# Sixteen more attention steps transpose the probabilities by DMA, two weight loads get another gate, and a few instructions change places

## The chip, the cores and the metric

The kernel runs on one core of one Trainium2 chip. The metric is the device time of one execution in microseconds. The kernel before took 1331.49 us (median of 3 runs, 1330.44 to 1332.63). The execution that the profiler recorded took 1330.85 us, of which the profiled span is 1329.0 us.

## The reference

The input `x` has 8 batches of 128 tokens with 512 features, and a context of the same shape. Two layers follow each other, each with a cross attention and a feed-forward part:

```python
x = x + tanh(g_xattn[0]) * xattn_0(layernorm(x), ctx)   # 32 query heads, 8 key/value heads of 128
x = x + tanh(g_ffn[0])   * ffn_0(layernorm(x))          # blockwise 4- and 6-bit rounded weights and inputs
x = x + tanh(g_xattn[1]) * xattn_1(layernorm(x), ctx)
x = x + tanh(g_ffn[1])   * ffn_1(layernorm(x))          # int4 weights, permuted inputs, bias
```

Each attention projects q from the normalised `x` and k and v from the context, normalises each head of q and k (RMS), takes softmax(q k^T / sqrt(128) + mask) v, and multiplies the result with the output weights.

## The kernel before

**Steps.** One unit of attention is one group (one key/value head and its 4 query heads) of one batch. There are 2 x 8 groups x 8 batches = 128 units, and the kernel runs one step per unit, in a software pipeline: step n projects k, v and q of unit n, computes the scores and the softmax of unit n-1, turns the probabilities of unit n-2 and multiplies them with v, and multiplies unit n-3 with the output weights. Every projection is three products of two halves of a float (`three_products`, L1276): upper times upper, lower times upper, upper times lower.

**Stages.** `run_steps` gives each step a kind. FIRST is steps 0 to 7. QUANT is a loop over steps 8 to 47, which also quantises the feed-forward weights. ZONE is steps 48 to 87, written out one by one; there the order of the units is `ZONE_ORDER`, so that layer 0's feed-forward part can run between them. PLAIN is a loop over steps 88 to 119. LAST is steps 120 to 127, written out, and the drain behind it (steps 128 to 133), in which the last feed-forward part runs as well.

**The feed-forward part in the zone.** Steps 56 to 74 carry one tile (batch) of it in two steps, by the class `Tiles`: a `gate` step (odd) runs the gate and up products for columns 0 to 1023, and the `down` step behind it (even) the rest of them and the product with the down weights (L1448, 11 matmuls, written `ITILES`). The quantised input of a tile is transposed by a DMA from ACT's queue (`f_xqT`, L738), the hidden values by three DMAs (`f_iqT`, L685, for matmuls 0 to 3, 4 to 7 and 8 to 10). ACT issues both in the order of its program.

**Weights.** They arrive in two slots by DMA from SP's queue (`load_group`), and ACT and POOL split them into the halves (`split_upper` L710, `split_lower` L531). The tables `SPLIT_ZONE` and `SPLIT_ZONE_LATE` say which pieces are split in which step of the zone; pieces 0 to 5 of a group are q, k and v, pieces 6 to 9 are the output weights. In the zone the output weights of the next group wait for the slot (`y_ps`) and also for the third (or fifth) `f_iqT` of the last chunk, `iT_sb[2]` (L435). The q, k and v loads of the group after it stand behind them on SP.

**The transpose of the probabilities.** In FIRST, QUANT, ZONE and LAST, PE does it: four transposes into the bank `psPO` (`probabilities`, L1333), which ACT copies to `pT_hi` (L771), and DVE subtracts to `pT_lo` (L1012). In PLAIN a DMA does it. DVE scales the probabilities (L995) and copies their upper and lower 16 bits to two planes `p_planes` (L1002, two copies), SP issues the transpose (L498), ACT puts the upper halves back into `p_whole` (L762) and DVE the lower ones (L1007), ACT rounds `p_whole` to `pT_hi` (L766), and DVE subtracts (`probs_lower`). `by_dma(kind)` tells which way is taken. SP's loop `plain_group` has a load of q, k and v ahead of the group's first transpose and the load of the output weights behind the fourth.

**PE's order in a step.** k and v, q, (gate and up 2 in `down` steps), probabilities' transposes, scores (L1340), (gate and up 0), output (L1276), then `transposed()`: k's transpose (L1357) and q's four (L1268), then `values()` (L1369, three matmuls with `pT_hi` and `pT_lo`), and last gate and up 1 or the down product. In steps 124 on, `last_x` transposes the tile that is normalised for the last feed-forward part, right behind q; from step 125 `final` multiplies one tile behind `values`.

**DVE's order in a step.** In PLAIN: reciprocal (L986), scaling (L995), planes (L1002), `oT_lo` (L1065), `v_lo` (L1082), masked scores (L1109), `p_whole` (L1007), maximum (L990), q normalised (`scaled_q`, L1020), `pT_lo` (L1012), kT (L1135), x (L1147). In steps 124 to 127 the moments of a tile (L865) come behind `oT_lo` and its normalisation (L871) behind `v_lo`, and the scaling of the probabilities comes behind the moments. ACT copies that tile's transpose (`xT_hi`, L669) ahead of the normalised k (L699).

Of the kernel before, what the change touches and what calls it, by code (L numbers as in the profile page):

```python
# [4 lines left out]
FP32 = mybir.dt.float32  # L5
# [10 lines left out]
P = 128  # L16
# [51 lines left out]
LAST0 = ALL - BATCHES  # L68
END = ALL + 6
# [26 lines left out]
def step_of(group, b):  # L96
# [4 lines left out]
              13: ((C, 0), (C, 1)), 15: ((C, 4), (C, 5)), 17: ((C, 8), (C, 9)), 19: ((E, 2), (E, 3)), 21: ((E, 6), (E, 7)),  # L101
# [4 lines left out]
SPLIT_ZONE_LATE = {13: ((C, 2), (C, 3)), 15: ((C, 6), (C, 7)), 17: ((E, 0), (E, 1)), 19: ((E, 4), (E, 5)),  # L106
# [49 lines left out]
def flamingo_kernel(nc, x, ctxT, mask, g_xattn, g_ffn, norms, wq, wk, wv, wo, ffn_w,  # L156
                    packedT, scalesT, perm, bias, w4_rows, out):
    top = ExitStack()
    with top:
# [50 lines left out]
        p_turned = sb("p_turned", [P, 2 * KT, P], U16, under)  # L210
        p_whole = sb("p_whole", [P, D], FP32, under)
# [155 lines left out]
        def by_dma(kind):  # L367

            return kind == PLAIN

        def turned_by_pe(n):

            return n - 1 - (LAST0 - ZONE1 if isinstance(n, int) and n >= LAST0 else 0)

# [22 lines left out]
        def _(sp):  # L397
# [16 lines left out]
            def load_group(before, slot, q=None, freed=None, downs=None):  # L414
# [49 lines left out]
            load_group(B, 0, None, step_of(A, BATCHES - 1) + 1, 3)  # L464
            load_group(C, 1, None, step_of(B, BATCHES - 1) + 1, 5)
# [18 lines left out]
            def plain_group(before, slot):  # L484

                g, at = before + 1, slot * WSLOT
                for b in range(BATCHES):
                    unit = before * BATCHES + b - ZONE1
# [5 lines left out]
                    sp.wait_ge(planes_done, unit + 1)  # L494
                    sp.wait_ge(upper_placed, unit + 1)
                    sp.wait_ge(lower_placed, unit + 1)
                    sp.sem_inc(turning, 1)
                    sp.dma_start_transpose(p_turned[:, :, :], p_planes[:, :]).then_inc(planes_turned, 16)  # L498
# [3 lines left out]

            with sp.Fori(GROUPS // 2 + 1, GROUPS - 1) as h:
                plain_group(h * 2 + 1, 0)
                plain_group(h * 2 + 2, 1)
# [146 lines left out]
        def _(act):  # L652
# [59 lines left out]
            def step(n, b, kind, j, q=None):  # L712
# [19 lines left out]
                split_upper(late_pieces(n, kind))  # L732
                if calm(n, kind):
                    split_upper(split_pieces(n, b, kind, j))
# [23 lines left out]
                if has(n, 2) and by_dma(kind):  # L758

                    act.wait_ge(pv_ps, n - 2)  # L760
                    act.wait_ge(planes_turned, (n - ZONE1 + 1) * 16)
                    nc.scalar.activation(halves(p_whole[:, :])[:, :, 1], p_turned[:, 0:KT, :].rearrange("p k t -> p (k t)"),  # L762
                                         ACT.Copy).then_inc(upper_placed, 1)
                    act.wait_ge(upper_placed, n - ZONE1 + 2)
                    act.wait_ge(lower_placed, n - ZONE1 + 2)
                    nc.scalar.activation(pT_hi[:, :], p_whole[:, :], ACT.Copy).then_inc(pt_hid, 1)  # L766
                if has(n, 2) and not by_dma(kind):
# [52 lines left out]
                for k in gathered(n, kind):  # L820

                    act.wait_ge(w4_back, 16)
                    nc.scalar.activation(wp_hi[:, k, :], w4_turned[:, k, :], ACT.Copy).then_inc(wp_hid, 1)
# [29 lines left out]
        def _(dve):  # L853
# [151 lines left out]
            def place_lower(n):  # L1005
                dve.wait_ge(planes_turned, (n - ZONE1 + 1) * 16)
# [3 lines left out]
            def probs_lower(n, kind=None):  # L1010
                dve.wait_ge(pt_hid, n - 1)
                nc.vector.tensor_tensor(pT_lo[:, :], (p_whole if by_dma(kind) else psPO)[:, :], pT_hi[:, :].bitcast(FP32),  # L1012
# [28 lines left out]
            def step(n, b, kind, j, q=None):  # L1041
# [9 lines left out]
                if by_dma(kind):  # L1051
                    scaled_probs(n)
                    probs_planes(n)
# [23 lines left out]
                if has(n, 2) and not t.active and not by_dma(kind):  # L1077
                    scaled_probs(n)
                if has(n, 0):
# [4 lines left out]
                    if t.first is not None:  # L1084
                        ctx_lower(t.first)
# [468 lines left out]
```

## Time and profile before

| what | value |
|---|---|
| median of 3 runs | 1331.49 us |
| the profiled execution | 1330.85 us, span 1329.0 us |
| PE busy | 1315.4 us (99% of the span) |
| DVE busy | 979.3 us (74%) |
| ACT busy | 853.1 us (64%) |
| POOL busy | 624.9 us (47%) |
| share of PE in the chain that ended last | 90% |
| PE idle by the list of waits, longest | 3.9 us for `f_xqT`, 1.6 us at the start, 1.1 us for `f_iqT` |

Busy time counts a matmul from its start to a modelled end, so two that follow each other overlap. What one piece of work costs on PE is read from the distance between the starts of successive rows. The chain that ended last tells which engine set the end of the kernel, and the list of waits tells what an engine stood still for.

### The profile page before, as it was taken

How to read it: one execution, taken by the hardware profiler on the slowest of the kernel's cores; microseconds unless marked ns; L12 is line 12 of the kernel's file. 1: busy time of each engine (PE TensorE's matmuls, PEld its weight loads, DVE VectorE, ACT ScalarE, POOL GpSimd, SP SyncE). 2: the span in 40 equal slices, each digit the busy share in tenths (PEclk: the TensorE clock that was granted, in tenths of full speed). 3: DMA queues.
4: the chain of work that ended last, by engine and by line, in shares of the span. 5: the costliest groups of instructions: out<-in, count | busy, mean ns of one | idle time of the engine just before them, and what ended most of it. 6: DMA issues, size and time to landing. Idle time of an engine off the chain costs nothing.

```text
span 1329.0 us, 25509 instructions
## 1 busy us (share of the span) xinstructions
PE 1315.4 (99%) x7561; PEld 1113.1 (84%) x7561; DVE 979.3 (74%) x2055; ACT 853.1 (64%) x3339; POOL 624.9 (47%) x683
## 2 busy tenths in 40 slices
PE   8999999999999999999899999999999999999999
PEld 7888888888888888877677788888888888888887
DVE  6778787887878788688778857676767667675656
ACT  5767677676767676646566556666767667676542
POOL 2546565555555666357577534532333323232132
PEclk9999999999999999999999999999999999999999
DMA  8011211211121110021310012212232221320001
GB/s 295 1 60 51 68 49 26 74 38 63 50 66 51 66 51 27 5 67 23 95 51 16 20 48 68 92 64 64 57 80 55 58 54 53 79 55 16 1 9 56
DMA packets 83982, 73.90 MB, mean 56 GB/s; under 512 B 53185, under 2 KB 74561, under 8 KB 79809
## 3 DMA queue, kind: packets, MB, share of 16 engines
q1 hardware_dynamic: 66912, 67.46, 16.9%
q10 hardware_dynamic: 16672, 4.46, 1.6%
q0 software_dynamic: 320, 1.05, 0.2%
q8 instruction: 37, 0.61, 0.2%
q14 instruction: 41, 0.33, 0.1%
HBM read 57.48 MB, written 3.15 MB: 46 GB/s over the span
## 4 chain that ended last, share of the span: by engine, by line
PE 90%; DVE 4%; DMA 2%; POOL 2%; issue 1%; ACT 1%; SPq 0%; POOLq 0%; DVEq 0%; ACTq 0%
PE bank L1276 64%; PE bank L1340 8%; PE bank L1268 7%; PE bank L1369 7%; PE bank L1302 2%; PE bank L1357 1%; DMA f_iqT<-f_iq 1%; PE bank L1448 1%; DMA w_raw<-in_wv 1%; POOL rstd L560 0%; DMA f_xqT<-f_xq 0%; DVE f_q L955 0%; DVE amax L948 0%; POOL f_iq L586 0%; POOL probs L597 0%
## 5 line engine op out<-in xcount | busy, mean ns | idle before, releaser
L531 POOL TENSOR_TENSOR w_lo<-w_raw,w_hi (+1 forms) x150 | 196.7, 1327 | 150.5 <-ACT w_hi L710 150.5
L745 ACT ACTIVATE squares<-bank 128x128 bf16<-128x128 f32 x512 | 134.8, 279 | 197.7 <-PE bank L1276 197.4
L1109 DVE SCALAR_TENSOR_TENSOR probs<-bank,mask_sb 128x512 f32<-128x512 f32 x127 | 87.6, 690 | 191.0 <-PE bank L1340 173.5
L691 ACT ACTIVATE probs<-probs,negmax 128x128 f32<-128x128 f32 x512 | 198.2, 391 | 6.3 <-DVE negmax L990 3.8
L556 POOL TENSOR_TENSOR meansq<-sumsq,scalars 128x5 f32<-128x5 f32 x128 | 27.5, 215 | 370.5 <-ACT squares L745 370.5
L560 POOL TENSOR_TENSOR rstd<-meansq,scalars 128x5 f32<-128x5 f32 x128 | 153.1, 1196 | 10.9 <-POOL meansq L556 1.3
L1276 PE MATMUL bank<-w_hi,oT_hi 128*128 (+1 forms) x512 | 152.0, 419 | 0.0
L1276 PE MATMUL bank<-w_hi,xT_hi 128*128 (+1 forms) x512 | 141.2, 396 | 0.3 <-ACT w_hi L660 0.2
L1276 PE MATMUL bank<-w_hi,oT_lo 128*128 (+1 forms) x512 | 138.0, 391 | 0.0
L1276 PE MATMUL bank<-w_lo,oT_hi 128*128 (+1 forms) x512 | 137.9, 391 | 0.0
L1276 PE MATMUL bank<-w_lo,xT_hi 128*128 (+1 forms) x512 | 137.5, 390 | 0.1
L1276 PE MATMUL bank<-w_hi,xT_lo 128*128 (+1 forms) x512 | 137.0, 389 | 0.0
L1340 PEld LDWEIGHTS bank<-kT,qT 128*128 128x128 f32 x1024 | 130.5, 191 | 6.4
L1340 PE MATMUL bank<-kT,qT 128*128 128x128 f32 x1024 | 134.8, 274 | 0.0
L1276 PEld LDWEIGHTS bank<-w_lo,oT_hi 128*128 128x128 f32 x512 | 96.4, 188 | 22.0
L1276 PEld LDWEIGHTS bank<-w_lo,xT_hi 128*128 128x128 f32 x512 | 96.1, 188 | 21.9 <-DVE w_lo L884 0.7
L1276 PEld LDWEIGHTS bank<-w_hi,oT_lo 128*128 128x128 f32 x512 | 96.1, 188 | 21.2
L1276 PEld LDWEIGHTS bank<-w_hi,xT_lo 128*128 128x128 f32 x512 | 96.1, 188 | 19.9
L745 ACT ACTIVATION_READ_ACCUMULATOR squares<-bank 128x1 f32 x512 | 106.6, 208 | 0.0
L1276 PEld LDWEIGHTS bank<-w_hi,xT_hi 128*128 128x128 f32 x512 | 88.0, 189 | 13.2 <-ACT w_hi L660 1.4
L1276 PEld LDWEIGHTS bank<-w_hi,oT_hi 128*128 128x128 f32 x512 | 88.1, 191 | 12.7 <-issue 0.3
L691 ACT ACTIVATION_READ_ACCUMULATOR probs<-probs,negmax 128x1 f32 x512 | 97.3, 190 | 0.0
(129 smaller groups left out, 2986.0 us busy)
## 6 DMA issues: line engine op xcount, KB each, us to landing
w_raw<-in_wq SPq DMA_DIRECT2D x16, 1024.0 KB, 4.9
w_raw<-in_wo SPq DMA_DIRECT2D x16, 1024.0 KB, 4.9
fw_raw<-in_ffn_w SPq DMA_DIRECT2D x36, 192.0 KB, 2.3
w_raw<-in_wk SPq DMA_DIRECT2D x16, 256.0 KB, 5.3
w_raw<-in_wv SPq DMA_DIRECT2D x16, 256.0 KB, 5.5
x_sb<-in_x SPq DMA_DIRECT2D x7, 256.0 KB, 10.6
ctx_raw<-in_ctxT SPq DMA_DIRECT2D x7, 256.0 KB, 10.4
fw_raw<-in_ffn_w SPq DMA_DIRECT2D x7, 256.0 KB, 2.7
```

Of the source, the lines that this page charges most:

```text
L531: last = nc.gpsimd.tensor_tensor(lo, raw, hi.bitcast(FP32), ALU.subtract)
L556: nc.gpsimd.tensor_tensor(meansq[:, :], sumsq[:, :], eps_sb[:, :], ALU.add).then_inc(ms_done, 1)
L560: nc.gpsimd.tensor_tensor(rstd[:, :], meansq[:, :], minus_half[:, :], ALU.pow).then_inc(rs_done, 1)
L691: last = nc.scalar.activation(probs[:, h * P:(h + 1) * P], probs[:, h * P:(h + 1) * P], ACT.Exp, bias=negmax[:, h:h + 1], accum_out=rowsum ...
L745: last = nc.scalar.activation(squares[:, h // 2, (b + 1) % 4, h % 2, :], q_bank(n, kind)[:, h * P:(h + 1) * P], ACT.Square, scale=SCALE, a ...
L1109: nc.vector.scalar_tensor_tensor(heads(probs[:, :]), heads(psSQ[:, :]), SCALE, mask_sb[:, :].unsqueeze(1).to_broadcast([P, REP, P]), ALU.m ...
L1268: last = nc.tensor.transpose(dst[:, k * P:(k + 1) * P], src[:, k * P:(k + 1) * P], m)
L1276: last = nc.tensor.matmul(dst, left(a, k), right(b, k), start=(n == 0), stop=(n == len(terms) - 1))
L1302: last = nc.tensor.matmul(ps[:, 0:width], f_xqT[:, k, :], wT[:, col:col + width], start=(k == 0), stop=(k == KT - 1))
L1340: last = nc.tensor.matmul(psSQ[:, h * P:(h + 1) * P], qT[:, h * P:(h + 1) * P], kT[:, :], start=True, stop=True)
L1357: nc.tensor.transpose(kv_bank(n, kind)[:, 2 * P:3 * P], kn[:, :], ident[:, :]).then_inc(kt_ps, 1)
L1369: last = nc.tensor.matmul(psPO[:, :], v[:, slot, :], p[:, :], start=(k == 0), stop=(k == 2))
```

## The change

1. `DMA0 = ZONE1 - BATCHES` (step 80). `by_dma(n, kind)` is true for steps 80 to 127, so steps 80 to 87 (the end of the zone) and 120 to 127 (LAST) turn their probabilities by DMA as well. All counts that began at `ZONE1` begin at `DMA0`. SP runs `turning_group(E + 1, 1)` ahead of its loop and eight `turn_probs` behind it. A spacer moves `p_whole` off `f_s`.
2. PE's order in steps 80 to 127 is k's transpose, the values, q's transposes. DVE takes `probs_lower` ahead of `scaled_q` there.
3. In `down` steps of the zone `values()` stands between matmuls 7 and 8 of the down product.
4. The loads of the output weights for two groups of the zone wait for the fourth and the sixth `f_xqT`, not for the third and the fifth last `f_iqT`. Four pieces move: (C, 6) and (C, 7) from the late place of step 63 to step 65, (C, 8) and (C, 9) to the late place of 65, (E, 0) and (E, 1) from there to the late place of step 66.
5. The splits of the last feed-forward weights (`gathered`, steps 83 to 86) move from the end of the step to ahead of the scores on ACT and DVE, and the load of `w4_turned` moves on SP behind the transpose of step 81. The output weights that stood ahead of it now load behind the transpose of step 83.

```diff
+DMA0 = ZONE1 - BATCHES
-              13: ((C, 0), (C, 1)), 15: ((C, 4), (C, 5)), 17: ((C, 8), (C, 9)), 19: ((E, 2), (E, 3)), 21: ((E, 6), (E, 7)),
+              13: ((C, 0), (C, 1)), 15: ((C, 4), (C, 5)), 17: ((C, 6), (C, 7)), 19: ((E, 2), (E, 3)), 21: ((E, 6), (E, 7)),
...
-SPLIT_ZONE_LATE = {13: ((C, 2), (C, 3)), 15: ((C, 6), (C, 7)), 17: ((E, 0), (E, 1)), 19: ((E, 4), (E, 5)),
+SPLIT_ZONE_LATE = {13: ((C, 2), (C, 3)), 17: ((C, 8), (C, 9)), 18: ((E, 0), (E, 1)), 19: ((E, 4), (E, 5)),
                    21: ((E, 8), (E, 9))}
...
+        def by_dma(n, kind):
+            return kind == PLAIN or (isinstance(n, int) and DMA0 <= n < ALL)
...
-                    if downs is not None:
-                        sp.wait_ge(iT_sb[2], 16 * downs)
+                    if inputs is not None:
+                        sp.wait_ge(fxT_sb, 16 * inputs)
...
-            load_group(B, 0, None, step_of(A, BATCHES - 1) + 1, 3)
-            load_group(C, 1, None, step_of(B, BATCHES - 1) + 1, 5)
+            load_group(B, 0, None, step_of(A, BATCHES - 1) + 1, 4)
+            load_group(C, 1, None, step_of(B, BATCHES - 1) + 1, 6)
...
-            load_group(E + 1, 1)
-            sp.wait_ge(w4_scattered, 4 * 16)
-            sp.dma_start(w4_turned[:, :, :], w4_rows.rearrange("(k p) o -> p k o", p=P)).then_inc(w4_back, 16)
...
+            def turn_probs(n):
+                sp.wait_ge(planes_done, n - DMA0 + 1)
+                sp.wait_ge(upper_placed, n - DMA0 + 1)
+                sp.wait_ge(lower_placed, n - DMA0 + 1)
+                sp.sem_inc(turning, 1)
+                sp.dma_start_transpose(p_turned[:, :, :], p_planes[:, :]).then_inc(planes_turned, 16)
...
+                    turn_probs(before * BATCHES + b)
+                    if isinstance(before, int) and b == 1:
+                        sp.wait_ge(w4_scattered, 4 * 16)
+                        sp.dma_start(w4_turned[:, :, :], w4_rows.rearrange("(k p) o -> p k o", p=P)).then_inc(w4_back, 16)
...
+            turning_group(E + 1, 1)
             with sp.Fori(GROUPS // 2 + 1, GROUPS - 1) as h:
...
+            for n in range(LAST0, ALL):
+                turn_probs(n)
...
+                if by_dma(n, kind):
+                    probs_lower(n, kind)
                 if has(n, 2) and (t.gate is not None or calm(n, kind)):
                     probs_lower(n, kind)
...
-                if has(n, 0):
-                    transposed()
-                if has(n, 2):
+                if by_dma(n, kind):
+                    transposed_k()
+                    values()
+                    transposed_q()
+                elif has(n, 0):
+                    transposed_k()
+                    transposed_q()
+                if has(n, 2) and not by_dma(n, kind) and t.down is None:
                     values()
...
                     for k, (r, rows) in enumerate(ITILES):
+                        if k == CHUNKS[2][0] // P:
+                            values()
```

## Rows read from the trace of the kernel before

**Rows 1.** The page, part 1: busy us, share of span, instructions.
```profile
PE 1315.4 (99%) x7561; PEld 1113.1 (84%) x7561; DVE 979.3 (74%) x2055; ACT 853.1 (64%) x3339; POOL 624.9 (47%) x683
```

**Rows 2.** Waits of PE, whole span: us in total, times, longest us.
```profile
PE bank L1302 <- DMA f_xqT<-f_xq: 3.9, 1, 3.9
...
PE bank L1448 <- DMA f_iqT<-f_iq: 1.1, 1, 1.1
```

**Rows 3.** Timeline of PE, step 63: start us, us, engine, line, operation.
```profile
636.05 1.06 PE L1340 MATMUL bank<-kT,qT 128*128 128x128 f32 x8
...
646.17 1.07 PE L1276 MATMUL bank<-w_hi,oT_lo 128*128 128x512 f32 x4
```

**Rows 4.** Timeline of PE, step 65.
```profile
668.58 1.06 PE L1340 MATMUL bank<-kT,qT 128*128 128x128 f32 x8
...
673.04 1.07 PE L1276 MATMUL bank<-w_hi,oT_lo 128*128 128x512 f32 x4
```

**Rows 5.** Busy us by engine in a stretch, then granted clock, DMA share, GB/s.
```profile
643.10:646.20 3.10, 3.10 (x11) 2.46 (x10) 2.69 (x7) 1.41 (x8) 0.00 (x0) 0.63 0.00 0
```

**Rows 6.** Timeline of ACT and SP, step 63.
```profile
634.99 0.63 ACT L710 ACTIVATE w_hi<-w_raw 128x512 fp32r<-128x512 f32 x1 [1.39 <-DMA w_raw<-in_wo]
635.05 1.21 ACTq L738 DMA_TRANSPOSE f_xqT<-f_xq  x1
...
635.86 0.33 SPq L405 DMA_DIRECT2D w_raw<-in_wq  x1
```

**Rows 7.** The tile f_xqT: its 8 transposes, issue to landing.
```profile
DMA to landing us min/median/max: 2.4/2.4/5.9
```

**Rows 8.** Timeline of PE, a step whose probabilities PE transposes.
```profile
905.14 0.27 PE L1357 MATMUL bank<-ident,kn 128*128 128x128 f32 x1
...
905.61 0.48 PE L1369 MATMUL bank<-pT_hi,v_hi 128*128 128x512 f32 x1
905.92 0.39 PE L1369 MATMUL bank<-pT_lo,v_hi 128*128 128x512 f32 x1
...
906.38 0.65 PE L1276 MATMUL bank<-w_hi,ctx_hi 128*128 128x256 f32 x4
...
914.67 0.27 PE L1357 MATMUL bank<-ident,kn 128*128 128x128 f32 x1
```

**Rows 9.** Timeline of PE, a PLAIN step.
```profile
933.39 0.27 PE L1357 MATMUL bank<-ident,kn 128*128 128x128 f32 x1
...
934.00 0.50 PE L1369 MATMUL bank<-pT_hi,v_hi 128*128 128x512 f32 x1
...
934.80 0.63 PE L1276 MATMUL bank<-w_hi,ctx_hi 128*128 x4
...
942.60 0.27 PE L1357 MATMUL bank<-ident,kn 128*128 128x128 f32 x1
```

**Rows 10.** Timeline of ACT and DVE, the same PLAIN step.
```profile
932.10 0.63 ACT L766 ACTIVATE pT_hi<-p_whole 128x512 fp32r<-128x512 f32 x1 [0.32 <-DVE p_whole L1007]
...
932.65 0.69 DVE L1020 TENSOR_TENSOR qn<-bank,rstd 128x512 f32<-128x512 f32 x1
...
933.26 0.68 DVE L1012 TENSOR_TENSOR pT_lo<-p_whole,pT_hi 128x512 fp32r<-128x512 f32 x1
...
935.71 0.76 DVE L1002 COPY p_planes<-probs 128x512 uint16<-128x512 uint16 x2
```

**Rows 11.** The tile p_turned: ns min/median/max, first and last start; landing.
```profile
L762 ACT ACTIVATE p_whole<-p_turned x32: 787/799/820, 922.5 to 1208.0; 128x512 uint16<-128x512 uint16 x32
...
DMA to landing us min/median/max: 3.0/3.0/4.8
```

**Rows 12.** Timeline of DVE and PE, step 124.
```profile
1251.36 0.68 DVE L865 BATCH_NORM_STATS2 ln_stats<-x_sb 128x6 f32<-128x512 f32 x1
...
1253.57 0.55 DVE L871 TENSOR_SCALAR f_s<-x_sb,ln_mv,ln_rstd 128x512 f32<-128x512 f32 x1 [0.53 <-POOL ln_rstd L544]
...
1254.17 0.65 PE L1268 MATMUL bank<-ident,f_s 128*128 128x128 f32 x4
```

More of the change, by code:

```diff
@@ L365, in qn_first @@
             return kind == FIRST or calm(n, kind) or t.down is not None or t.next is not None
-        def by_dma(kind):
-            return kind == PLAIN
+        def by_dma(n, kind):
+            return kind == PLAIN or (isinstance(n, int) and DMA0 <= n < ALL)
         def turned_by_pe(n):
-            return n - 1 - (LAST0 - ZONE1 if isinstance(n, int) and n >= LAST0 else 0)
+            return n - 1 - (ALL - DMA0 if isinstance(n, int) and n >= ALL else 0)
         def halves(ap):
@@ L732, in step @@
                 split_upper(late_pieces(n, kind))
+                for k in gathered(n, kind):
+                    act.wait_ge(w4_back, 16)
+                    nc.scalar.activation(wp_hi[:, k, :], w4_turned[:, k, :], ACT.Copy).then_inc(wp_hid, 1)
                 if calm(n, kind):
@@ L1011, in probs_lower @@
                 dve.wait_ge(pt_hid, n - 1)
-                nc.vector.tensor_tensor(pT_lo[:, :], (p_whole if by_dma(kind) else psPO)[:, :], pT_hi[:, :].bitcast(FP32),
+                nc.vector.tensor_tensor(pT_lo[:, :], (p_whole if by_dma(n, kind) else psPO)[:, :], pT_hi[:, :].bitcast(FP32),
                                         ALU.subtract).then_inc(pt_lod, 1)
@@ L1076, in step @@
                     row_inverse(n)
-                if has(n, 2) and not t.active and not by_dma(kind):
+                if has(n, 2) and not t.active and not by_dma(n, kind):
                     scaled_probs(n)
@@ L1085, in step @@
                         ctx_lower(t.first)
+                for k in gathered(n, kind):
+                    dve.wait_ge(wp_hid, k + 1)
+                    nc.vector.tensor_tensor(wp_lo[:, k, :], w4_turned[:, k, :], wp_hi[:, k, :].bitcast(FP32),
+                                            ALU.subtract).then_inc(wp_lod, 1)
                 if t.first is not None:
@@ L1104, in step @@
                     dve.wait_ge(s_ps, n)
[L1105 to L1106 removed]
+                    if by_dma(n, kind):
+                        dve.wait_ge(planes_done, n - DMA0 + 1)
                     else:
@@ L1111, in step @@
                         mask_sb[:, :].unsqueeze(1).to_broadcast([P, REP, P]), ALU.mult, ALU.add).then_inc(masked, 1)
-                if by_dma(kind):
+                if by_dma(n, kind):
                     place_lower(n)
@@ L1115, in step @@
                     maximum(n)
+                if by_dma(n, kind):
+                    probs_lower(n, kind)
                 if has(n, 2) and (t.gate is not None or calm(n, kind)):
@@ L1125, in step @@
                     maximum(n)
-                if has(n, 2) and t.gate is None and not qn_first(n, kind, t):
+                if has(n, 2) and t.gate is None and not qn_first(n, kind, t) and not by_dma(n, kind):
                     probs_lower(n, kind)
@@ L1165, in step @@
                     int4_weights(n - INT4_0)
-                for k in gathered(n, kind):
-                    dve.wait_ge(wp_hid, k + 1)
-                    nc.vector.tensor_tensor(wp_lo[:, k, :], w4_turned[:, k, :], wp_hi[:, k, :].bitcast(FP32),
-                                            ALU.subtract).then_inc(wp_lod, 1)
                 if kind == LAST and n == LAST0:
@@ L1364, in values @@
                     pe.wait_ge(pt_lod, n - 1)
-                    if by_dma(kind):
+                    if by_dma(n, kind):
                         pe.wait_ge(o_lod, n - 2)
@@ L1385, in step @@
                     output()
-                    transposed()
+                    transposed_k()
+                    transposed_q()
                     values()
@@ L1412, in step @@
                     scores()
-                if has(n, 2) and not by_dma(kind):
+                if has(n, 2) and not by_dma(n, kind):
                     probabilities()
@@ L1433, in step @@
                     output()
-                if has(n, 0):
-                    transposed()
-                if has(n, 2):
+                if by_dma(n, kind):
+                    transposed_k()
+                    values()
+                    transposed_q()
+                elif has(n, 0):
+                    transposed_k()
+                    transposed_q()
+                if has(n, 2) and not by_dma(n, kind) and t.down is None:
                     values()
```

36 lines of the change are left out of this document (13 added, 23 removed).

## The prediction

> **What bounds the kernel now.** I read the page first, then the waits of PE, then the timelines of single steps. The page shows PE busy for 99% of the span and DVE, the next one, for 74% [rows 1]. So nearly every microsecond that PE saves comes off the end, and work that the change gives DVE or ACT is free until it makes PE wait. The waits of PE say how little idle time there is to win: one of 3.9 us for the transposed input of the feed-forward part, and one of 1.1 us for its hidden values [rows 2]. The rest must come from PE's own instructions. The working is therefore a comparison of step lengths, from k's transpose of one step to that of the next.
>
> **The stall in step 63.** From the scores to the last part of the output product takes 646.17 - 636.05 = 10.12 us in step 63 [rows 3] and 673.04 - 668.58 = 4.46 us in step 65 with the same work [rows 4]. The stall costs 5.66 us, more than the wait of 3.9 us. The clock shows the difference: after the idle time it is granted at 0.63 on average over 643.1 to 646.2, a mix of the 1.2 and the 2.4 GHz level, though PE is busy all through [rows 5]. Two things made the transpose late. ACT stood 1.39 us for the output weights ahead of it, and SP issued q's and k's weights 0.81 us after it [rows 6], and it took 5.9 us to land where the median is 2.4 us [rows 7]. The change takes away both: no piece is split at the late place of step 63, and the loads wait for this very transpose. It is then issued about 1.4 us earlier, near 633.6, lands by 636.0, and PE wants it at 636.05 + 0.9 = 637.0. What is late next is nothing within 1 us. The loads start near 636 and need some 6 us; the first transpose behind them is one step later, and the first consumer two steps later. The same holds for the second moved load. Taken: -5.6 us. Bounds: -1 us (only ACT's wait of 1.39 us goes) and -5.7 us.
>
> The four moved pieces are as many as before. In step 66 ACT gets two more of 0.6 us each [rows 6]. They fall between v and q's squares, where it waits for PE (ACT is busy for 64% [rows 1]), so I cost them at nothing. Without that cover the transposes behind them would be late by 1.2 us, the upper end.
>
> **Values inside the down product.** Eight steps. The eight matmuls ahead of the values now cover the wait for `pT_lo`, some 0.15 us as in a PLAIN step (below), but the step from bf16 to the split products, and back, is paid one more time. I take 0; bounds -1.5 and +1.5 us for the eight. The wait of 1.1 us in step 66 [rows 2] stays: the last three matmuls wait for the same landing, wherever the values stand.
>
> **PE's transposes of the probabilities.** From the first k and v product to k's next transpose is 914.67 - 906.38 = 8.29 us with them [rows 8] and 942.60 - 934.80 = 7.80 us without [rows 9]. So each of the 16 steps saves 0.49 us there, 7.8 us in all.
>
> **The new end of a step.** k's transpose to the first product of the next step takes 906.38 - 905.14 = 1.24 us where PE transposes [rows 8], and 934.80 - 933.39 = 1.41 us in PLAIN [rows 9]. The values begin 0.47 us after k's transpose in the one and 0.61 us in the other. The cause is `pT_lo`, which ends at 933.26 + 0.68 = 933.94, 0.06 us ahead of the values [rows 9, 10]. With `pT_lo` ahead of q on DVE it can start once `pT_hi` is there (932.10 + 0.63 = 932.73) and ends near 933.45. k's transpose takes 0.11 us, so the values start 0.14 us after it. q is then ready near 934.1, before the values end. The wait is gone but for 0.03 us.
>
> The new order has a price. The first values matmul behind q's transposes takes 905.92 - 905.61 = 0.31 us, and the next two 0.46 / 2 = 0.23 us each [rows 8]: the change from transposes to split products costs 0.08 us. The old order has it once, the new one twice (k's transpose to the values, q's transposes to the next product). I take 0.1 us for the second. The step's end is then 1.41 - 0.12 + 0.10 = 1.39 us. That is 0.02 to 0.03 us less than now in the 32 PLAIN steps (-0.9 us) and 0.15 us more than in a step with PE's transposes (16 x 0.15 = +2.4 us). Bounds: 0 and 0.2 us for the second change, that is -4.8 and +4.8 us over 48 steps.
>
> The Trainium skill (TensorE: Matmul & The Clock Gate, section Step-by-step: what each phase is for) says that the next weight load is pulled ahead of running matmuls, so that it overlaps them. By this rule the second change of kind is free, and the sum would be the rival at 1317.7 us below. The 0.08 us of the rows above speak against it for this pair of kinds; for a k and v product behind transposes no row exists.
>
> **What the DMA way adds to DVE, ACT and SP.** Two copies to planes (0.76 us) [rows 10], `p_whole`'s upper half on ACT (0.80 us) [rows 11] and its lower half. In PLAIN these fit a period of (1208.0 - 922.5) / 31 = 9.21 us [rows 11]. The planes end at 935.71 + 0.76 = 936.47, and 0.1 us for SP and 3.0 us later, at 939.6, the transpose lands. ACT begins `p_whole` at 932.10 - 0.32 - 0.80 = 930.98 [rows 10, 11], so a period later, at 940.2. That is 0.6 us of slack. The new order makes DVE 0.15 us later, and some 0.45 us remain. In steps 83 to 86 the gathered weights add 0.6 us on ACT and on DVE between v and the scores, where both wait for PE. The load of q, k and v stands ahead of the transpose of step 80 as in PLAIN. The first transpose took longer, 4.8 us [rows 11], and I expect 0.3 to 0.4 us for it again, at step 80 and no more at step 88. In straight-line code a few more transposes may be late: +0.4 us for the 16 steps. Bounds: -0.2 and +6 us.
>
> **Steps 124 to 127.** Here the order on DVE bites. The chain from moments to `last_x` on PE is 1254.17 - 1251.36 = 2.81 us, and PE starts 0.05 us after the normalisation ends (1253.57 + 0.55) [rows 12], so it has no slack. The DMA way puts the scaling (0.7 us, today behind the moments) and the planes (0.76 us [rows 10]) ahead of it, and starts DVE's step later. My estimate: DVE comes to the reciprocal 1.6 us after k's transpose of step 123, and gap, scaling, planes and `oT_lo` take 0.2 + 0.7 + 0.7 + 0.6 us, so the moments start at 3.8 us (today 2.7) and `last_x` is ready at 6.6 us. PE is there after 5.5 to 5.6 us, as today: a wait of 1.0 us. In step 125, with `xT_lo` ahead as well, it is 1.1 to 1.2 us. Steps 126 and 127 have 2.7 us of final products ahead and hide it. ACT's copy of the turned tile now stands between `pT_hi` and k, which makes k's transpose some 0.3 us late in each of the four steps. Together +3.3 us; bounds 0 and +6 us.
>
> **The sum.** -5.6 (step 63), 0 (down steps), -7.8 (transposes), +2.4 and -0.9 (new end of a step), +0.4 (late landings), +3.3 (steps 124 to 127), and -0.4 for the later start that moves from step 88 to step 80 and its partly smaller price: -8.6 us. On the profiled execution's 1330.85 us that is 1322.3 us. The median of the runs is 0.6 us above that execution; I forecast 1322.5 us.
>
> **Rivals.**
> 1. The second change of kind is free. For it: weight loads overlap elsewhere. Against it: the 0.08 us of rows 8. Then 48 x 0.1 us less, 1317.7 us.
> 2. The input's transpose in step 63 stays late, because a wait other than the weights holds ACT or the loads find another transpose to delay. Against it: its landing is at the median wherever no load runs beside it. Then only some 1 us of 5.6 us comes, and the time is 1327 us; with the last steps at their upper bound 1330 us.
> 3. Slower: the DMA transposes in the 16 straight-line steps land late. The slack is about 0.45 us over 3.0 us; each further microsecond is PE's. At the 4.8 us of the worst one [rows 11] a step loses 4.8 - 3.45 = 1.35 us, 16 steps 21.6 us, and the time is 1322.5 + 21.6 - 0.4 = 1343.7 us. It decides from a mean landing near 4.0 us, where 16 x 0.55 us eat the gain. Against it: the median is 3.0 us, and the 1.5 MB of loads ahead of a group's first transpose do not move it.
> 4. The values or q's transposes wait in the new order because `pT_hi` comes from ACT later than I read. At 0.15 us a step, 48 steps cost 7 us: 1329.5 us, no measurable change.
>
> **Chances.** The forecast 0.60, rival 1 0.18, rival 2 0.09, rival 3 0.05, rival 4 0.08. What a measurement can tell from no change is 0.2%, 2.7 us, so "faster" is below 1328.8 us. The forecast and rival 1 are faster, rival 2 half of the time or more: 0.86 with a part of rival 4. Within 0.2%: 0.09. Slower: 0.05. The range of 8 in 10 goes from 1316 us, past rival 1, to 1328 us.
>
> **What would show it.** The wait of PE for `f_xqT` is gone and the clock is full throughout. Steps 80 to 86 and 120 to 122 are 9.15 to 9.20 us long instead of 914.67 - 905.14 = 9.53 [rows 8], and PLAIN's 9.17 to 9.21. The first k and v product behind q's transposes takes 0.08 us or more over its group of today. PE waits for `f_s` in steps 124 and 125. The prediction is wrong if PLAIN's step falls below 9.12 us or rises above 9.25 us, if the last steps lose nothing, or if `p_turned` has a median landing above 3.4 us.

## The result and the profile after

| | before | after |
|---|---|---|
| median of 6 runs, us | 1330.68 (1329.57 to 1332.63) | 1326.87 (1325.66 to 1327.81) |
| ratio to before, 95% interval | | 0.9969 [0.9956, 0.9982] |
| profiled execution: span, us | 1329.0 | 1325.3 |

The change made the kernel 3.8 us (0.3%) faster. That lies in the forecast range (1316 to 1328 us), but it is less than half of the 8.6 us of the sum. The page of the changed kernel, part 1, answers to [rows 1]:

```profile
PE 1308.3 (99%) x7497; PEld 1103.1 (83%) x7497; DVE 994.0 (75%) x2103; ACT 864.3 (65%) x3355; POOL 623.2 (47%) x683
```

PE has 64 transposes less and is busy 7.1 us less, yet the span shrank by only 3.65 us (1329.00 to 1325.35): PE now waits more. The waits of PE (us in total, times, longest) answer to [rows 2]:

```profile
PE bank L1469 <- issue: 3.6, 7, 0.5
PE bank L1367 <- ACT kn L707: 2.4, 4, 1.0
PE bank L1497 <- POOL ident L530: 1.6, 1, 1.6
PE bank L1278 <- DVE f_s L879: 1.3, 2, 0.8
...
PE bank L1381 <- DVE pT_lo L1020: 0.6, 2, 0.3
...
PE bank L1469 <- DMA f_iqT<-f_iq: 0.4, 1, 0.4
```

The wait of 3.9 us for `f_xqT` is gone. In its place stand a wait called "issue" ahead of the down product, seven times 0.5 us, and waits for `kn`, `f_s` and `pT_lo`. The wait for `f_iqT` fell from 1.1 to 0.4 us in this execution, but that is no finding: in e3 and e4, which have the same code in the zone, it is 1.0 us and none.

The difference in step lengths says what each stretch gave. The length of step n runs from its own transpose of k to that of step n+1, so it holds the rest of step n and most of the work of step n+1:

| steps | forecast, us | measured, us |
|---|---|---|
| 0 to 56 | 0 | +0.27 |
| 56 to 79 (step 63, down steps) | -5.6 | -3.25 |
| 79 to 88 (8 new DMA steps) | -2.7 | -3.10 |
| 88 to 119 (PLAIN) | -0.9 | +0.19 |
| 119 to the end (8 new DMA steps) | +0.6 | +2.16 |
| start of the span | 0 | +0.08 |
| sum | -8.6 | -3.65 |

The late landings (+0.4) and the late first transpose (-0.4) of the forecast cancel and stand in no line. The readings behind this table follow.

**Step 63.** Timeline of PE (start us, us), which answers to [rows 3], and the transposed input's landing, to [rows 7]:

```profile
636.88 1.06 PE L1350 MATMUL bank<-kT,qT 128*128 128x128 f32 x8
637.77 1.89 PE L1312 MATMUL bank<-wT,f_xqT 128*128 128x512 bf16 x8
...
641.34 1.07 PE L1286 MATMUL bank<-w_hi,oT_lo 128*128 128x512 f32 x4
```
```profile
DMA to landing us min/median/max: 2.4/2.4/2.5
```

From the scores to the last part of the output product are now 641.34 - 636.88 = 4.46 us, as in the undisturbed step of [rows 4], where [rows 3] had 10.12 us. The stretch from the scores to k's transpose runs at the full clock (0.63 before [rows 5]), though DMA is busy for 0.91 of it:

```profile
636.88:642.25 5.37, 5.37 (x31) 3.96 (x30) 4.18 (x7) 3.90 (x19) 2.61 (x4) 1.00 0.91 316
```

**A step with a down product (64).** DVE and PE, start, length, and in brackets the idle time before:

```profile
655.08 0.68 DVE L1020 TENSOR_TENSOR pT_lo<-bank,pT_hi 128x512 fp32r<-128x512 f32 x1
...
655.31 0.63 PE L1278 MATMUL bank<-ident,qn 128*128 128x128 f32 x4
655.68 0.68 DVE L885 TENSOR_TENSOR xT_lo<-bank,xT_hi 128x512 fp32r<-128x512 f32 x1
656.46 1.89 PE L1469 MATMUL bank<-wT,f_iqT 128*128 128x512 bf16 x8 [0.52 <-issue]
658.00 0.58 PE L1381 MATMUL bank<-pT_hi,v_hi 128*128 128x512 f32 x1
```

The down product writes the bank from which DVE still subtracts to get `xT_lo`. PE starts 0.10 us after that subtraction ends (655.68 + 0.68 = 656.36). The view names no engine for this semaphore and calls the time "issue". Before, the values products stood between q's transposes and the down product, and their 0.8 us covered the wait. That `xT_lo` is what PE waits for is inferred here from the two times; e1 and e2 test it.

**A written-out step with the DMA way (83).** Timeline of PE, which answers to [rows 8]:

```profile
871.94 0.30 PE L1367 MATMUL bank<-ident,kn 128*128 128x128 f32 x1
872.01 0.47 PE L1381 MATMUL bank<-pT_hi,v_hi 128*128 128x512 f32 x1
...
872.78 0.60 PE L1278 MATMUL bank<-ident,qn 128*128 128x128 f32 x4
873.14 0.72 PE L1286 MATMUL bank<-w_hi,ctx_hi 128*128 128x256 f32 x4
873.70 0.64 PE L1286 MATMUL bank<-w_lo,ctx_hi 128*128 128x256 f32 x4
874.17 0.64 PE L1286 MATMUL bank<-w_hi,ctx_lo 128*128 128x256 f32 x4
...
881.03 0.29 PE L1367 MATMUL bank<-ident,kn 128*128 128x128 f32 x1
```

The step takes 881.03 - 871.94 = 9.09 us, against 9.53 us in [rows 8]. The first four k and v products behind q's transposes take 873.70 - 873.14 = 0.56 us, the next four 0.47 us: the second change of kind costs 0.09 us. In e5 the same four products stand behind the values and take 865.82 - 865.34 = 0.48 us, so the price comes from what stands ahead of them and not from their being the first:

```profile
865.34 0.65 PE L1284 MATMUL bank<-w_hi,ctx_hi 128*128 128x256 f32 x4
865.82 0.64 PE L1284 MATMUL bank<-w_lo,ctx_hi 128*128 128x256 f32 x4
```

A PLAIN step takes 9.18 us, against 9.21 us in [rows 9]:

```profile
1002.13 0.27 PE L1367 MATMUL bank<-ident,kn 128*128 128x128 f32 x1
1002.24 0.50 PE L1381 MATMUL bank<-pT_hi,v_hi 128*128 128x512 f32 x1
...
1011.31 0.27 PE L1367 MATMUL bank<-ident,kn 128*128 128x128 f32 x1
```

**Step 124.** PE, POOL, DVE and ACT, which answer to [rows 12]:

```profile
1247.47 0.66 PE L1278 MATMUL bank<-ident,f_s 128*128 128x128 f32 x4 [0.53 <-DVE f_s L879]
...
1249.62 1.29 POOL L653 TENSOR_TENSOR x_sb<-x_sb,bias_sb 128x512 f32<-128x512 f32 x1
1249.66 1.57 DVE L1015 COPY p_whole<-p_turned 128x512 uint16<-128x512 uint16 x1
1251.33 0.63 ACT L778 ACTIVATE pT_hi<-p_whole 128x512 fp32r<-128x512 f32 x1 [2.54 <-DVE p_whole L1015]
1252.76 0.33 PE L1367 MATMUL bank<-ident,kn 128*128 128x128 f32 x1 [0.98 <-ACT kn L707]
```

The wait for `f_s` is there, at half the forecast size. Larger is one that the forecast did not have: DVE's copy of the turned tile's lower half takes 1.57 us where its median is 0.46 us. It starts 0.04 us after POOL's addition of the bias and ends 0.32 us after it (1249.62 + 1.29 = 1250.91; 1249.66 + 1.57 = 1251.23). `pT_hi`, k and k's transpose come late behind it. Step 123 to 124 takes 11.46 us instead of 10.09, step 124 to 125 11.70 instead of 10.15.

**Late landings.** Where a turned tile lands late, ACT shows it (step 95):

```profile
981.33 0.79 ACT L774 ACTIVATE p_whole<-p_turned 128x512 uint16<-128x512 uint16 x1 [1.07 <-DMA p_turned<-p_planes]
...
983.09 0.33 PE L1367 MATMUL bank<-ident,kn 128*128 128x128 f32 x1 [0.38 <-ACT kn L707]
```

The two lengths around such a landing both grow, the first because k waits and the second because the values start late. Steps 85 and 86 take 9.57 and 9.50 us, 0.48 and 0.40 us more than the steps ahead of them; steps 94 and 95 take 9.74 and 9.87 us, 0.57 and 0.69 us more than theirs. The landing of the 48 transposes is otherwise as in [rows 11]:

```profile
DMA to landing us min/median/max: 3.0/3.0/4.7
```

### The profile page after: what moved, and what is told of

Read it like the earlier page. It is cut to its first block, busy times and chain, and to the rows that moved or that the text cites. A ratio compares the mean times of both kernels' runs of the same rounds, so it can differ in the third digit from the quotient of the medians.

```text
span 1325.3 us, 25509 instructions
## 1 busy us (share of the span) xinstructions
PE 1308.3 (99%) x7497; PEld 1103.1 (83%) x7497; DVE 994.0 (75%) x2103; ACT 864.3 (65%) x3355; POOL 623.2 (47%) x683
## 3 DMA queue, kind: packets, MB, share of 16 engines
q10 hardware_dynamic: 16672, 4.46, 1.6%
## 4 chain that ended last, share of the span: by engine, by line
PE 88%; issue 5%; DVE 3%; POOL 1%; DMA 1%; ACT 1%; SPq 0%; POOLq 0%; ACTq 0%; DVEq 0%
PE bank L1286 62%; PE bank L1350 8%; PE bank L1278 7%; PE bank L1381 7%; PE bank L1312 2%; PE bank L1469 1%; PE bank L1367 1%; DMA p_turned<-p_planes 1%; POOL rstd L568 1%; DMA w_raw<-in_wv 1%; DVE probs L1122 0%; DVE pT_lo L1020 0%; ACT pT_hi L778 0%; DVE w_lo L892 0%; DVE p_whole L1015 0%
## 5 line engine op out<-in xcount | busy, mean ns | idle before, releaser
L539 POOL TENSOR_TENSOR w_lo<-w_raw,w_hi (+1 forms) x150 | 194.0, 1309 | 162.4 <-ACT w_hi L718 162.4
L568 POOL TENSOR_TENSOR rstd<-meansq,scalars 128x5 f32<-128x5 f32 x128 | 156.0, 1219 | 10.8 <-POOL meansq L564 1.1
```

What stands on the lines that cost most here:

```text
L539: last = nc.gpsimd.tensor_tensor(lo, raw, hi.bitcast(FP32), ALU.subtract)
L568: nc.gpsimd.tensor_tensor(rstd[:, :], meansq[:, :], minus_half[:, :], ALU.pow).then_inc(rs_done, 1)
```

## The experiments

Every median below is of 4 to 11 runs (e9: 4, e5: 11). The kernel before ran beside them, with medians of 1330.84 us (beside e1 to e4), 1330.69 us (e5 to e8) and 1330.08 us (e9, e10), and ratios are to it. Kernels of different groups are therefore compared by what each gained on the kernel before beside it. The 95% intervals of most ratios overlap with the change's, so what one edit did is read from the step lengths of the traces. Those have a spread of their own: the sum of steps 56 to 74 differs by up to 1.1 us between traces with the same code there (238.4 us in the change and e4, 239.5 us in e3), most of it in step 58, while steps 60, 62, 64, 70 and 72 agree within 0.03 us. Line numbers in a kernel move by up to 7 where lines were added; e6 has those of the kernel before.

**e6: the moved loads and splits alone.** The kernel before, with `SPLIT_ZONE`, `SPLIT_ZONE_LATE` and the wait of the change:

```
-                        sp.wait_ge(iT_sb[2], 16 * downs)
+                        sp.wait_ge(fxT_sb, 16 * inputs)
```

> The kernel before with the moved loads and pieces of the zone alone (the wait for the fourth and sixth input transpose, the tables of the splits). Theory: the whole stall of step 63, 5.1 to 5.7 us, is this part's, and nothing of it needs the DMA way: 1330.8 - 5.4 = 1325.4 us, and the interval 62 to 63 falls from 19.5 to 13.9 us. Rival (the moved loads meet another transpose): a new wait for f_iqT or f_xqT of over 1 us shows in steps 64 to 68, and the gain is under 4 us.

Measured: 1325.58 us, 0.9961 [0.9947, 0.9976]. The stretch from k's transpose of step 62 to that of step 63 falls from 19.50 to 13.84 us, by 5.66 us. The wait for `f_xqT` is gone, and one wait of 0.9 us for `f_q` came behind k's transpose of step 67, one step behind the place to which two of the pieces moved:

```profile
PE bank L1302 <- DVE f_q L955: 0.9, 1, 0.9
```

Steps 56 to 74 give 4.84 us together. This one edit carries a gain of about 5 us. The rest of the change gave nothing in sum: against e6 the trace of the change is 1.6 us longer from step 56 to 79, 3.1 us shorter from 79 to 88 and 2.2 us longer behind step 119. The edit moves the loads and the pieces together, so how much of the stall each of the two caused is not separated.

**e1: the values ahead of the down product again.**

```
-                if has(n, 2) and not by_dma(n, kind) and t.down is None:
+                if has(n, 2) and not by_dma(n, kind):
                     values()
-                        if k == CHUNKS[2][0] // P:
-                            values()
```

> The changed kernel with the values ahead of the down product again, as before. Theory: in the changed kernel the down product writes the bank that DVE still reads for xT_lo, and without the values ahead of it PE waits 0.5 us for that in each of the seven down steps that also have a next tile; those steps fall from 14.3 to 14.4 us to 13.9 us, and the time by 3.5 us, to about 1323.4 us. Rival, the time is lost in the three changes between bf16 and split products inside the down product: then step 58, which has no next tile, loses as well, the wait labelled issue remains in part, and the step falls by 0.2 us, the time by 1.5 us.

Measured: 1324.89 us, 0.9952 [0.9939, 0.9966], 2.0 us less than the change. The wait called "issue" is gone from PE's list, and steps 56 to 74 are 2.46 us shorter (3.5 us expected). The down steps 60, 62 and 64 take 13.84 us instead of 14.37 to 14.38, the steps behind them 13.06 instead of 12.92. PE in step 64:

```profile
654.15 0.63 PE L1278 MATMUL bank<-ident,qn 128*128 128x128 f32 x4
654.66 0.50 PE L1381 MATMUL bank<-pT_hi,v_hi 128*128 128x512 f32 x1
...
655.46 2.55 PE L1467 MATMUL bank<-wT,f_iqT 128*128 128x512 bf16 x11
```

**e2: the values stay inside, DVE takes `xT_lo` ahead of `pT_lo`.** This takes away the wait and keeps the order of the change on PE:

```
+                if t.next is not None and t.down is not None:
+                    xT_lower(BATCHES + t.next)
                 if has(n, 2) and qn_first(n, kind, t) and not calm(n, kind):
                     probs_lower(n, kind)
-                if t.next is not None:
+                if t.next is not None and t.down is None:
                     xT_lower(BATCHES + t.next)
```

> The changed kernel with one exchange on DVE in down steps: xT_lo of the next tile ahead of pT_lo. The values stay inside the down product. Theory (PE waits for xT_lo): the wait of 0.5 us shrinks to under 0.1 us, down steps fall to 13.8 to 13.9 us, the time by 3 to 3.6 us, to about 1323.5 us. Rival (the cost is the change of kind inside the down product): down steps keep 14.3 us and the time stays at 1326.9 us.

Measured: 1324.94 us, 0.9955 [0.9941, 0.9968]. DVE and PE in step 64:

```profile
653.67 0.68 DVE L885 TENSOR_TENSOR xT_lo<-bank,xT_hi 128x512 fp32r<-128x512 f32 x1
...
653.90 0.63 PE L1280 MATMUL bank<-ident,qn 128*128 128x128 f32 x4
...
654.27 0.68 DVE L1020 TENSOR_TENSOR pT_lo<-bank,pT_hi 128x512 fp32r<-128x512 f32 x1
654.45 1.89 PE L1471 MATMUL bank<-wT,f_iqT 128*128 128x512 bf16 x8
```

The product starts 0.55 us after q's transposes began, without a gap. Steps 56 to 74 are 3.00 us shorter than in the change and 0.54 us shorter than in e1; its down steps 60, 62, 64 and 70 take 13.76 to 13.80 us, those of e1 13.84 us. So the cost was the wait for `xT_lo` and not the extra changes between bf16 and the split products: with the wait gone, the values inside are the slightly better place. e2's time is no better than e1's because one more transpose landed late in it, the one of step 84 (4.45 us): steps 79 to 87 are 1.2 us longer than in the change and 0.6 us longer than in e1.

**e3: PE transposes the probabilities again from step 124 on.**

```
-            return kind == PLAIN or (isinstance(n, int) and DMA0 <= n < ALL)
+            return kind == PLAIN or (isinstance(n, int) and DMA0 <= n < LAST0 + 4)
```

The count of PE's own transposes and SP's loop go with it.

> The changed kernel with the DMA way for steps 80 to 123 alone; steps 124 to 127 transpose on PE again, with the order of before. Theory: steps 124 and 125 lose 2.9 us in the changed kernel against before, the two behind them and the drain about 0.8 us, all by DVE's planes and POOL's bias; they come back: 1326.9 - 3.5 = 1323.4 us, and the intervals 123 to 124 and 124 to 125 return to 10.1 us. Rival (the loss comes from what lies ahead of step 124, a late transpose or the new end of a step): the two intervals stay over 11 us.

Measured: 1323.62 us, 0.9945 [0.9932, 0.9959]. Step 119 to the end of the span is 117.7 us long, against 120.7 us in the change and 118.6 us before. The DMA way in the last four steps thus costs 3 us against PE's. The two stretches named in the expectation take 10.66 and 10.16 us; the first stays 0.6 us above the 10.1 us, with a wait of 0.46 us for `f_s` in it.

**e4: POOL's addition of the bias waits for `pT_lo`.** The DMA way stays in the last steps; only what runs beside DVE's copy and subtraction moves:

```
                     pool.wait_ge(bias_ready, 1)
+                    if n < ALL:
+                        pool.wait_ge(pt_lod, n - 1)
```

> The changed kernel with POOL's addition of the bias in steps 124 to 127 held back until pT_lo of the step is done. Theory: DVE's copy into p_whole (1.57 and 1.29 us in steps 124 and 125 instead of 0.46) and its pT_lo (1.32 us in 126 and 127 instead of 0.68) are slow because POOL's addition runs at the same time on tiles in SBUF; they return to 0.46 and 0.68 us, k's transpose is late by 0.3 us at most instead of 1.0 and 0.7, and the time falls by 1.5 to 2.3 us, to about 1325 us. Rival (the copy waits for something else, such as the landing of the transpose): both durations stay.

Measured: 1323.56 us, 0.9942 [0.9928, 0.9955]. DVE's copy in step 124:

```profile
1249.53 0.45 DVE L1017 COPY p_whole<-p_turned 128x512 uint16<-128x512 uint16 x1
```

It takes 0.45 us instead of 1.57, and the longest of all 48 is 0.47 us. Steps 119 to the end take 117.6 us, as in e3. The waits for `f_s` stay (1.4 us in two). So of the loss in the last steps about 3 us were POOL's addition beside DVE, which the forecast had not seen, and 1.4 us the late `f_s`, which it had at 2.1 to 2.2. The repair gave more than the 1.5 to 2.3 us expected of it, since the waits for `kn` (1.67 us in two) and for `pT_lo` (0.56 us in two) went as a whole and the stretch behind step 127 is 0.65 us shorter too.

**e5: the order of PE and DVE as before, the DMA way in all 48 steps.**

```
                     transposed_k()
-                    values()
                     transposed_q()
+                    values()
```

On DVE `pT_lo` goes behind q's scaling again.

> The changed kernel with the order of before in all 48 DMA steps: k's transpose, q's transposes, the values on PE, and q ahead of pT_lo on DVE. Theory: the new order takes away the wait for pT_lo (0.14 us) and pays a second change from transposes to split products (0.09 us), so it is worth 0.05 us in a PLAIN step and 0.12 us in a step written out; without it PLAIN steps are 9.22 us again and the written-out ones 9.2 us, the time rises by 3 to 4 us, to 1330.3 us. Rival (the new order is worth nothing, since q's transposes then stand late and the step's end moves on): no step changes by more than 0.03 us and the time stays at 1326.9 us.

Measured: 1327.47 us, 0.9981 [0.997, 0.9992]. PLAIN steps take 9.23 us as before, but the written-out steps 80 to 84 take 9.49 to 9.53 us, nearly as much as with PE's transposes (9.53), and not the 9.2 us expected. POOL and DVE in such a step of e5:

```profile
861.72 1.44 POOL L568 TENSOR_TENSOR rstd<-meansq,scalars 128x5 f32<-128x5 f32 x1
861.72 0.46 DVE L1015 COPY p_whole<-p_turned 128x512 uint16<-128x512 uint16 x1
...
863.19 0.69 DVE L1028 TENSOR_TENSOR qn<-bank,rstd 128x512 f32<-128x512 f32 x1 [0.46 <-POOL rstd L568]
```

and POOL in a PLAIN step of it:

```profile
927.78 1.17 POOL L568 TENSOR_TENSOR rstd<-meansq,scalars 128x5 f32<-128x5 f32 x1
```

There the copy starts 0.09 us later (927.87), and `rstd` takes 1.17 us; where both start together it takes 1.44 us, q and k wait for it, and so does PE. Both orders show the same lengths of `rstd`. In the traces of the change and of e5 it takes 1.44 to 1.48 us in all 21 cases in which the two start together, and 1.17 us in all 61 in which the copy starts 0.09 to 0.10 us later. After the late landing of step 86 in e5 `rstd` takes 1.17 us, and the step behind it takes 9.10 us instead of 9.50. The new order puts `pT_lo` into the gap on DVE and the values into the one on PE, and the step takes 9.09 us. The two parts of the change only pay together: the DMA way alone gives 0.03 us a step here, both together 0.44 us.

The time rose by 0.6 us against the change and not by the 3 to 4 us expected. From step 79 to 88 the old order is 2.25 us longer, but from 88 to 119 only 0.27 us, since a late landing costs it less (the section on the prediction has the numbers), and from 119 to the end it is 1.25 us shorter. In step 124 DVE's copy comes 0.17 us ahead of POOL's addition there and takes 0.45 us. So the new order pays in the steps written out in the zone and up to step 122; from step 123 on, with POOL's addition where it stood, it costs 2.3 us.

**e10: the DMA way in steps 80 to 119 only, with e2's edit.**

```
-            return kind == PLAIN or (isinstance(n, int) and DMA0 <= n < ALL)
+            return kind == PLAIN or (isinstance(n, int) and DMA0 <= n < LAST0)
```

The count of PE's own transposes and SP's loop go with it here too.

> The changed kernel with xT_lo ahead of pT_lo in down steps, and no DMA way in steps 120 to 127 (steps 80 to 119 alone). Theory: the DMA way in steps 120 to 127 is worth +0.5 us (step 120) + 3 x 0.35 us, and costs 2.9 us in 124 and 125 and 0.8 us behind, so without it the time falls from 1324.9 us to about 1322.7 us. Rival (the DMA way pays in LAST as a whole): the time rises above 1324.9 us.

Measured: 1321.91 us, 0.9938 [0.9925, 0.9952]. The medians of e2 and e10 are 3.0 us apart, but they come from different groups; against the kernel before beside it e10 gained 2.3 us more than e2 (2.2 us expected), and in the traces the stretch from step 119 to the end is 2.2 us shorter. Steps 119 to 122 lose 0.44, 0.45, 0.30 and 0.32 us by it, steps 123 and 124 win 2.9 us. As changed, the last eight steps by the DMA way were thus a loss on the whole, though four of them gained. With POOL's addition held back they are a gain: the same stretch takes 117.6 us in e4 and 118.5 us in e10.

**e7: e2's and e4's edits together.** Neither touches the other's steps, so that they should add up.

> The changed kernel with two of the repairs together: xT_lo ahead of pT_lo in down steps, and the bias held back in steps 124 to 127. Theory: the two causes are independent and add: 1326.9 - 2.5 - 2.8 = 1321.6 us. Rival (they share PE time, one wait taking the place of the other): only the larger of the two gains shows, 1323.6 us.

Measured: 1321.64 us, 0.9936 [0.9921, 0.9951]: 5.2 us less than the change, so the two add.

**e8: e7, and the moments ahead of the scaling and the planes on DVE in steps 124 to 127.**

```
-                if by_dma(n, kind):
+                if by_dma(n, kind) and t.last is None:
                     scaled_probs(n)
                     probs_planes(n)
```

Both calls follow `moments(...)` in those steps.

> As the kernel with both repairs, and in steps 124 to 127 DVE takes the moments of the tile ahead of the scaling and the planes, as before. Theory: PE's waits for f_s in steps 124 and 125 (0.5 and 0.8 us) go, but the planes are 1.0 us later there, with 0.45 us of slack, so about 0.5 us a step comes back as a wait for p_turned: net -0.3 us, 1321.3 us. Rival (the planes' chain has more slack than that): both waits go and nothing comes, 1320.3 us. Other side: the late planes delay k as well, through ACT's order, by 0.9 us a step: 1322 us.

Measured: 1322.61 us, 0.994 [0.9926, 0.9953], 1.0 us more than e7. That is within the spread of e7's runs (1320.05 to 1324.55 us), but the trace agrees: the stretch from step 119 to the end is 0.85 us longer. The waits for `f_s` fall only from 1.4 to 1.1 us, and k's transpose waits 0.44 and 0.40 us where it did not wait in e7, the "other side" of the expectation; step 123 to 124 goes from 10.34 to 11.02 us.

**e9: e7, and PE transposes `f_s` behind the scores.** Not DVE's order moves but the place where PE asks:

```
-                if t.last is not None and n < ALL:
-                    last_x(t.last)
                 ...
                 if has(n, 1) and not calm(n, kind):
                     scores()
+                if t.last is not None and n < ALL:
+                    last_x(t.last)
```

> As the kernel with both repairs, and in steps 124 to 127 PE transposes the normalised tile behind the scores, not ahead of them. Theory: DVE's normalisation ends 0.5 and 0.8 us after PE is there in steps 124 and 125; the scores take 0.8 us and cover both waits, so they go: 1321.6 - 1.3 = 1320.3 us. Rival (what PE saves there it loses at k's transpose, because ACT's copy of the turned tile then stands 0.8 us later ahead of k): the waits for k grow by as much and the time stays at 1321.6 us.

Measured: 1318.04 us, 0.9909 [0.9894, 0.9923], the fastest: 12.0 us less than the kernel before beside it, where e7 has 9.0 us. PE in step 124:

```profile
1245.45 1.05 PE L1354 MATMUL bank<-kT,qT 128*128 128x128 f32 x8
1246.34 0.60 PE L1282 MATMUL bank<-ident,f_s 128*128 128x128 f32 x4
```

Both waits for `f_s` are gone, no wait for k came in their place, and steps 123 and 124 take 9.57 and 9.54 us (10.34 and 10.87 in e7). That is 2.1 us, and 2.5 us for the stretch from step 119 to the end, where 1.3 us were expected; what gave the rest is open. In its profiled execution steps 48 to 56 were 1.3 us longer and it took 1320.22 us; its other runs go down to 1317.33 us.

## Why the prediction was right in part

- **The stall in step 63: right.** Forecast -5.6 us; 5.66 us in e6, and 10.12 to 4.46 us in the change. The granted clock was 0.63 behind the idle time and is 1.00 without it, and counting that (5.66 us and not the wait's 3.9) was right. Not counted was a wait for `f_q` in step 67: 0.2 to 0.9 us in every trace with the moved pieces and none before. The two pieces that moved to step 66 are the likely cause, as the upper end of the bounds had it, but no run moves them alone.
- **Values inside the down product, "I take 0; bounds -1.5 and +1.5 us": the step that failed.** The forecast priced what PE gains and pays in changes of kind and did not ask what the down product itself waits for. It writes a bank that DVE reads until `xT_lo` is done, and the values products had hidden that. PE waited seven times 0.5 us for it; e1 and e2 both find 2.5 to 3.0 us in steps 56 to 74, outside the bounds. The list of waits before could not warn: a wait that is covered is in no list. What the forecast did price, the changes of kind, was right to be put near nothing, as e2 shows.
- **PE's transposes and the new end of a step: right.** Forecast -0.34 us a written-out step and -0.03 us in PLAIN; measured -0.44 and -0.04 (the medians of PLAIN are 9.22 and 9.18 us). Steps 80 to 84 take 9.07 to 9.13 us, a little under the 9.15 to 9.20 us named as a sign. The change of kind behind q's transposes costs 0.09 us (forecast 0.1), so rival 1, that it is free, is refuted. That the old order would have taken most of the gain in the written-out steps (9.50 us, e5) was not foreseen; that the forecast came near there is luck in part. By the Trainium skill (TensorE: Matmul & The Clock Gate, section Step-by-step: what each phase is for) the next weight load is pulled ahead of running matmuls. The trace agrees with that much, for the first load of the split products starts at 873.11 us, with the last of q's transposes; what was wrong was to read from it that the change of kind is free.
- **Late landings: the size was off.** Forecast +0.4 us in the 16 new steps and nothing in PLAIN. Steps 85 and 86 lost 0.9 us, steps 94 and 95 lost 1.3 us, and PLAIN's -0.9 us went that way. The transposes of steps 86 and 95 land late (4.4 to 4.7 us) in every trace with the DMA way from step 80 on, those of 84 and 93 in some. What they cost depends on the order: at the same landing of 4.4 us for step 95, steps 94 and 95 lose 0.2 us in e5 (old order) and 0.9 us in e3 (new order). The forecast took the new order's loss of slack, 0.15 us, as harmless. Why they land late is open. In the twelve traces 51 transposes take over 3.2 us, and beside every one of them a packet of the instruction queues runs between issue and landing; of the 481 others this holds for 29. No run was made on it.
- **Steps 124 to 127, "+3.3 us": direction right, content wrong.** `f_s` was late by 0.53 and 0.81 us and not by 1.0 and 1.1 to 1.2. k's transpose waits 0.98 and 0.69 us there, and the values 0.28 us in the two steps behind; POOL's addition beside DVE makes these, as e4 shows. Without it the stretch from step 119 to the end takes 117.6 us, 1.0 us less than before and 1.6 us better than the forecast's +0.6; with it 2.2 us more than before. So the terms that the forecast had were 1.6 us too high in this stretch, and one of 3.2 us was missing; that the two offset each other by half is luck.
- **Rivals 2 to 4 did not come.** `f_xqT` lands in 2.4 us, `p_turned`'s median stayed at 3.0 us, and PLAIN's step became shorter. No bound named as a refutation was crossed: the errors were in places for which no sign had been named.
- **The total.** The down steps (+2.4 us), the last steps (+1.6 us) and PLAIN (+1.1 us) make up the 5 us between the sum and the measurement; the other stretches cancel. The measured 1326.87 us lies in the range because the range reached up to 1328 us, not because the sum was near. The forecast also has a slip of 0.4 us: 1322.3 us for the profiled execution and 0.6 us for the median make 1322.9 us, not 1322.5.

The Trainium skill (SBUF — State Buffer, section Who interferes with whom) says that a DVE copy in a two-port mode, or a DVE instruction with two inputs in SBUF, shares a port pair with POOL, and that the one issued second is blocked until the first is done. The traces agree with it. In step 124 the copy of 0.46 us starts second and ends 0.32 us after POOL's addition, and in step 126 the subtraction with both inputs in SBUF takes 1.32 us instead of 0.69 and ends 0.56 us after it. Before, DVE's q (`qn`, one input in PSUM) took its usual 0.68 us wholly beside the same addition, and so did `pT_lo`, which read PSUM then and overlapped it by up to 0.23 us. The forecast listed what each engine gets to do; it did not ask where the operands had moved.

## What to carry to other kernels

When a block moves past another on an engine, list the waits that the block stood in front of: each one it covered can come back (here 0.5 us seven times), and the list of waits before does not show it. When an operand moves from PSUM to SBUF, look at what POOL runs at that moment. Where a chain on a second engine has become late, ask first whether the first engine can want its result later (e9, some 2.5 us less than e7) before reordering the second (e8, some 1 us more).

## What the runs showed of the hardware

- A copy or subtraction of 128x512 on DVE whose operands lie in SBUF is held up by POOL's addition of 1.29 us: 0.46 to 1.57 us, 0.69 to 1.32 us. DVE in step 126, beside POOL:

```profile
1275.53 1.29 POOL L653 TENSOR_TENSOR x_sb<-x_sb,bias_sb 128x512 f32<-128x512 f32 x1
...
1276.06 1.32 DVE L1020 TENSOR_TENSOR pT_lo<-p_whole,pT_hi 128x512 fp32r<-128x512 f32 x1 [0.20 <-ACT pT_hi L778]
```

- The other way round, POOL's `rstd` of 128x5 takes 1.44 to 1.48 us when DVE's copy starts together with it, and 1.17 us when the copy starts 0.09 us later (e5 and the change).
- A DMA transpose of the planes takes 3.0 us from issue to landing, and over 3.2 us (up to 4.8) only where a packet of the instruction queues runs beside it (51 of 51 in twelve traces; not shown to be the cause).
- Going from fp32 transposes to split products costs PE 0.09 us behind q's transposes, 0.56 against 0.47 us for the first four products of 256 columns, and 0.08 us for the first values product before [rows 8].
